# Mamba scan block: order of matmuls, vector work and activations within a tile, and where the scan's carry is kept

## The reference: what is computed

```
u  = silu(conv(in_proj_u(x)));  z = in_proj_z(x)
dt, B, C = split(x_proj(u));    dt = softplus(dt_proj(dt) + dt_b)
h[d,n] = exp(dt[d]*A[d,n]) * h[d,n] + dt[d]*u[d] * B[n]     # one step of time
y[d]   = sum_n h[d,n]*C[n] + u[d]*D[d]
out    = out_proj(y * silu(z))
```

## Time and profile before

| | |
|---|---|
| median of 3 runs | 1975.07 us (1973.82 to 1977.28) |
| profiled execution | 1973.6 us, of which the span from first to last instruction is 1971.8 us |
| busy in the span | PE 1445.4 us (73%), DVE 1359.6 (69%), POOL 1138.6 (58%), ACT 928.1 (47%) |
| granted TensorE clock, mean | 0.878 |
| Mamba block of layer 0, first to last scan | 56.5 to 588.6 us |
| Mamba block of layer 1, first to last scan | 1069.5 to 1602.2 us |

### The profile page before, as it was taken

The page is one execution under the profiler, slowest core; times in us unless marked ns, Lnnn a source line. Parts: engine busy times, 40 slices in busy tenths (PEclk is TensorE's granted clock), DMA queues, the critical chain, the costliest instruction groups (busy, mean ns, idle before and its releaser), DMA issues. The chain is left out here.

```text
span 1971.8 us, 28551 instructions
## 1 busy us (share of the span) xinstructions
PE 1445.4 (73%) x7776; PEld 980.9 (50%) x7777; DVE 1359.6 (69%) x1913; ACT 928.1 (47%) x1695; POOL 1138.6 (58%) x788
## 2 busy tenths in 40 slices
PE   6666766667656599999956766666667662799993
PEld 4333333333314499999834333333333222799992
DVE  2899999999995422222143999999999967444443
ACT  6666677667743011111136666677666731011111
POOL 0687788888880244444302888888878850355540
PEclk9889898998968699999968788998998866899996
DMA  3655566555638110111034565566555634111114
GB/s 110 147 135 121 129 144 146 125 126 134 145 79 354 54 41 32 38 37 36 26 126 98 129 138 121 129 143 139 134 121 135 148 136 188 38 48 48 47 41 152
DMA packets 75964, 217.61 MB, mean 110 GB/s; under 512 B 11856, under 2 KB 27408, under 8 KB 72592
## 3 DMA queue, kind: packets, MB, share of 16 engines
q1 hardware_dynamic: 67664, 194.53, 38.9%
q0 software_dynamic: 8256, 22.56, 3.5%
HBM read 178.34 MB, written 38.70 MB: 110 GB/s over the span
## 5 line engine op out<-in xcount | busy, mean ns | idle before, releaser
L669 POOL TENSOR_TENSOR L_hc<-L_h,L_cbq 128x1536 f32<-128x1536 f32 x192 | 660.1, 3438 | 210.6 <-DVE L_h L587 207.5
L492 ACT ACTIVATE ps<-L_dwq,L_negA 128x384 f32<-128x384 f32 x768 | 426.7, 574 | 227.4 <-DVE L_h L587 215.5
L364 PE MATMUL ps<-L_hc,same 128*32 128x384 f32 x1536 | 190.0, 571 | 238.9 <-POOL L_hc L669 238.9
L574 DVE TENSOR_TENSOR L_dbu<-L_dwq,ps 128x768 f32<-128x768 f32 x288 | 270.7, 941 | 29.4 <-DVE L_carry L649 13.1
L587 DVE TENSOR_TENSOR_SCAN L_h<-ps,L_h,L_dbu 128x384 f32<-128x384 f32 x288 | 275.0, 1002 | 12.9 <-ACT ps L492 12.8
L587 DVE TENSOR_TENSOR_SCAN L_h<-ps,L_carry,L_dbu 128x384 f32<-128x384 f32 x288 | 274.2, 1001 | 6.5 <-DVE L_dbu L574 4.7
L364 PEld LDWEIGHTS ps<-L_hc,same 128*32 128x32 f32 x1536 | 31.5, 113 | 358.2 <-POOL L_hc L669 324.3
L1151 DVE COPY Xn<-L_w 128x2048 f32 x86 | 107.6, 1253 | 117.1 <-PE ps L1101 108.3
L1134 ACT ACTIVATE L0e_hT<-ps 128x512 f32<-128x512 f32 x86 | 51.3, 597 | 267.2 <-PE ps L1101 267.2
L678 POOL TENSOR_TENSOR L_dbp<-L_dwq,L_cbq 128x768 f32<-128x768 f32 x96 | 175.1, 1824 | 0.0
L323 PE MATMUL ps<-Xn,L_fold 128*128 (+1 forms) x480 | 103.3, 368 | 89.2 <-DVE L_dw L595 89.2
(11 more groups left out here) (278 smaller groups left out, 2301.4 us busy)
## 6 DMA issues: line engine op xcount, KB each, us to landing
L_dwq<-dw_rows SPq DMA_DIRECT2D x192, 384.0 KB, 6.2
L_cbq<-cb_rows SPq DMA_DIRECT2D x192, 240.0 KB, 9.9
dw_rows<-L_dw SPq DMA_DIRECT2D x48, 384.0 KB, 2.3
L_w<-in_up SPq DMA_DIRECT2D x16, 1024.0 KB, 11.7
L_w<-in_down SPq DMA_DIRECT2D x8, 1024.0 KB, 26.6
tok_rows<-Xn SPq DMA_DIRECT2D x6, 768.0 KB, 13.1
L0s_got<-results SPq DMA_DIRECT2D x18, 256.0 KB, 2.9
L1s_got<-results SPq DMA_DIRECT2D x18, 256.0 KB, 3.5
```

The costliest lines, as they stand in the source:

```text
L364: mm = nc.tensor.matmul(y_ps[g * QW:(g + 1) * QW, :], same[:, 0:QW], hc[:, (k % 2) * Q + g, :], start=False, stop=(k == Q - 1))
L492: nc.scalar.activation(da(r, c), dwq[:, r, c % Q, 0, :], ACT.Exp, scale=negA[:, 0, c:c + 1]).then_inc(sem["da"], 1)
L574: nc.vector.tensor_tensor(dbu[:, at:at + 2, :], dwq[:, r, 2 * i:2 * i + 2, 1, :], spread(b_ps(r, k)), ALU.mult).then_inc(sem["dbu"], 1)
L669: nc.gpsimd.tensor_tensor(hc[:, at:at + Q, :], h[:, Q * k:Q * k + Q, :], cbq[:, r, k, :].unsqueeze(1).to_broadcast([P, Q, T]), ALU.mult).t ...
```

## The change

Four edits in the Mamba block.

1. PE: `spread_b(t, r, 2)` goes from behind `u_in` to the head of the tile; `u_in` is split in two (parts 0 and 1, then parts 2 to 4) around `sum_y(t-1, 3)`; `z_in` goes behind `u_in`; `project_dt` and `project_bc` go ahead of `sum_y(t, 0)` and `spread_b(t+1, 0)`. `add_relu` and `add_log` are written at the end of a tile for tile t+2 instead of at the head for tile t+1 (and once ahead of tile 0).
2. DVE: `times_u` goes from behind scan 3 to behind scan 0, `gate` from behind scan 5 to behind scan 3.
3. ACT: the block of two table loads, `silu_z` and `silu_u` goes from behind decay 7 to behind decay 6 (`SILU_AT`).
4. `h` gets one more column per state, which holds the state after the global token. Even tiles read their initial column from `h` too: column T-1, or column T where an image begins. The copy and DVE's wait for it are gone, and `carry` is only a step of the set-up.

```diff
@@ mamba, buffers
-        carry = sb("carry", [P, 2, N])
+        carry = sb("carry", [P, N])
...
-        h = sb("h", [P, N, T])
+        h = sb("h", [P, N, T + 1])
@@ tensor block
             spread_b(0, 0, 1)
+            add_relu(1)
+            add_log(1)
             pe.wait_ge(s_tok, 7)
 
             def tile(t, r, img1, img2, more):
 
                 first = isinstance(t, int) and t == 0
+                spread_b(t, r, 2)
+                if more == 2:
+                    u_in(t + 2, img2, (0, 1))
+                if not first:
+                    sum_y(t - 1, 1 - r, Q - 1)
+                if more == 2:
+                    u_in(t + 2, img2, (2, 3, 4))
                 if more:
-                    add_relu(t + 1)
-                    add_log(t + 1)
                     pe.wait_ge(sem["bc_out"], t + 2)
                     wait(pe, sem["res"], t - 1)
                     z_in(t + 1, img1)
-                if not first:
-                    sum_y(t - 1, 1 - r, Q - 1)
-                if more == 2:
-                    u_in(t + 2, img2, range(5))
-                spread_b(t, r, 2)
                 skip(t, r)
-                sum_y(t, r, 0)
-                if more:
-                    spread_b(t + 1, 1 - r, 0)
                 if more == 2:
                     project_dt(t + 2, r)
                     pe.wait_ge(sem["zs"], t + 2)
                     project_bc(t + 2, r)
+                sum_y(t, r, 0)
+                if more:
+                    spread_b(t + 1, 1 - r, 0)
                 sum_y(t, r, 1)
...
                 sum_y(t, r, 2)
+                if more == 2:
+                    add_relu(t + 2)
+                    add_log(t + 2)
@@ scalar block
-                    if c == 7 and more:
+                    if c == SILU_AT and more:
@@ vector block, scan
-                first = h[:, c, T - 1:T] if slot is None else carry[:, slot, c:c + 1] if isinstance(slot, int) \
-                    else carry[:, bass.ds(slot, 1), c:c + 1].rearrange("p a n -> p (a n)")
-                nc.vector.tensor_tensor_scan(h[:, c, :], da(t % 2 if isinstance(t, int) else int(slot is None), c),
+                first = h[:, c, T - 1:T] if slot is None else h[:, c, T - slot:T - slot + 1] if isinstance(slot, int) \
+                    else h[:, c, bass.ds(T - slot, 1)]
+                nc.vector.tensor_tensor_scan(h[:, c, 0:T], da(t % 2 if isinstance(t, int) else int(slot is None), c),
@@ vector block, tile
                     scan(t, 2 * j, slot)
+                    if j == 0 and not last:
+                        times_u(t + 1, 1 - r, [(s_dw_row[r], 16 * (p + 1))])
                     scan(t, 2 * j + 1, slot)
-                    if j == 1 and not last:
-                        times_u(t + 1, 1 - r, [(s_dw_row[r], 16 * (p + 1))])
                     if not (isinstance(t, int) and t == 0):
-                        if j == 2:
+                        if j == 1:
                             gate(t - 1, 1 - r)
@@ vector block, pair
-                if not last:
-                    dve.wait_ge(sem["scan"], (2 * p + 2) * N)
-                    nc.vector.tensor_copy(carry[:, 1, :], h[:, :, T - 1]).then_inc(sem["carry"], 1)
-                    dve.wait_ge(sem["carry"], p + 2)
@@ gpsimd block, times_c
-                nc.gpsimd.tensor_tensor(hc[:, at:at + Q, :], h[:, Q * k:Q * k + Q, :],
+                nc.gpsimd.tensor_tensor(hc[:, at:at + Q, :], h[:, Q * k:Q * k + Q, 0:T],
```

More of the change, by code:

```diff
@@ L36 @@
 DA_RING = 3
+SILU_AT = 6
 PAD = 2
@@ L614, in _ @@
             dve.wait_ge(s_tok, 6)
-            nc.vector.tensor_tensor(carry[:, 1, :].rearrange("p (k g) -> p k g", k=Q),
+            nc.vector.tensor_tensor(carry[:].rearrange("p (k g) -> p k g", k=Q),
                                     m["ones"][:, 0:N].rearrange("p (k g) -> p k g", k=Q),
@@ L618, in _ @@
             dve.wait_ge(sem["carry"], 1)
-            nc.vector.tensor_tensor(carry[:, 0, :].rearrange("p (k g) -> p k g", k=Q),
-                                    carry[:, 1, :].rearrange("p (k g) -> p k g", k=Q),
+            nc.vector.tensor_tensor(h[:, :, T].rearrange("p (k g) -> p k g", k=Q),
+                                    carry[:].rearrange("p (k g) -> p k g", k=Q),
                                     ps[:, 5, Q:2 * Q].unsqueeze(1).to_broadcast([P, Q, Q]), ALU.mult).then_inc(s_tok, 1)
```

## The result

The changed kernel takes 2000.79 us (median of 4 runs, 1997.96 to 2006.85) against 1976.14 us (4 runs): a ratio of 1.013, 95% interval 1.0103 to 1.0158. It is slower by some 25 us, where 2017 us was forecast. The profiled execution took 1998.67 us with a span of 1996.8.

The account below looks back on a forecast made before the run. VectorE was taken to bound the kernel, at some 21.1 us of work a tile. 44 tiles x (23.35 - 22.37) = 43 us on top of the profiled 1973.6 us gave 2017 us, range 1988 to 2046.

Parts of the forecast that it names:

- That dt comes no earlier, and VectorE waits for it in nearly every tile: Ahead of `times_u`: DVE idles 1 to 3 us in nearly every tile, some 60 to 90 us in all.
- 12.43 us from scan 7 to dt at full clock: Chain from the end of scan 7 through POOL, PE and `take_dt` to the next tile's dt: 12.43 us, no link shortened.
- the term "I take 0" for the pitch: POOL reading `h` at pitch 385 instead of 384: 0 to 0.2 us a pass, 0 to 18 us in all, taken as 0.
- the circle: Loop of scan 7, POOL, PE, `take_dt`, `times_u` and scan 7 again, in which the delay of dt goes round.
- 10.07 us from `times_u` to scan 7: DVE from the start of `times_u` to the end of scan 7: 6.44 + 2.76 + 0.87 = 10.07 us in the new order.
- The stall ahead of scan 7, 0.3 us: DVE waits 0.3 us ahead of scan 7 for the decay behind the activation block; before, it waited ahead of scan 8.
- Half of the clock's excess, 0.5 us a tile: PE's dt matmuls: low clock makes the mean tile's dt about 1.0 us later; half, 0.5, is taken.
- The rival of the clock "as before or worse": Low clock on dt matmuls: 23.85 us a tile, +65, 2039 us; always low 24.55, +96, 2070; chance 0.30.
- The circle at full clock, 22.85 us: Mamba tile: 12.43 + 0.05 + 10.07 + 0.3 = 22.85 us against 22.37 before, 0.48 more.
- The removed 28.6 us are swallowed by the wait: DVE: 18.3 us for the copy and its wait plus 10.3 for the spread, all lost to the wait for dt.
- Sum: Over the loops, 44 tiles x (23.35 - 22.37) = 43 us more, 2017 us; ends cancel.
- the prediction's own sum for full clock: Rival, dt always at full clock: 22.85 a tile, 1995 us; without stall 22.55, 1982; chance 0.52 together with the forecast.

Follow-up runs that it names:

- a scan: Changed kernel with `times_u` one scan later, behind scan 1: 1971.27 us, ratio 0.999 to the kernel before.
- `dbp`: Changed kernel with both parts of `dbp` behind the first `times_c` on GpSimd: 1977.25 us, ratio 1.0023 to the kernel before.
- two sums: Changed kernel with the first two of dt's three sums (relu and log) ahead of the third `sum_y` on PE: 1941.13 us, ratio 0.9833 to the kernel before.
- the run with PE kept busy: Changed kernel with the next tile's first spread done four times and the second three times: 1966.62 us, ratio 0.9965 to the kernel before.

## Why the prediction was right, point by point

- *That dt comes no earlier, and VectorE waits for it in nearly every tile*: right, 44 of 44 tiles, 69.3 us where 60 to 90 were forecast, though 26 of the waits were 0.55 to 1.44 us long, near the lower end of the 1 to 3 us named. The experiments that shortened one link each (a scan, `dbp`, the clock, two sums) all shortened the tile.
- *12.43 us from scan 7 to dt at full clock*: 11.80 measured. The step that was mis-sized is the term "I take 0" for the pitch, between bounds of 0 and +0.2 us a pass: it was -0.27, twice in the circle, 24 us over 44 tiles. The bound from below left out a gain, and nothing in the trace before could show it.
- *10.07 us from `times_u` to scan 7*: 10.11 measured, with the stall in it.
- *The stall ahead of scan 7, 0.3 us*: nearly absent, the two scans there take 1.98 instead of 1.92 us. From the end of `take_dt` to the end of scan 7 the mean of the 44 tiles is 10.23 us where 10.42 was forecast, 0.2 us too high, 8 us in all.
- *Half of the clock's excess, 0.5 us a tile*: too little. Fast dt takes 3.7 us from the third `times_c` and the mean was 4.50, so 0.8; dt ran slow in 18 of 44 tiles, against 25 before. The low clock did fall on the second `sum_y` more (19 tiles against 13), behind 3.04 to 3.15 us of idle, as argued, but in 16 tiles it ran fast behind as much. The rival of the clock "as before or worse" did not come: the mean granted clock is 0.880 against 0.878.
- *The circle at full clock, 22.85 us, already slower than the 22.37 before*: wrong, and the forecast of the sign leaned on it. In the run with PE kept busy, where dt is fast in all 44 tiles, the mean tile is 22.09 us and the kernel 0.35% faster than the one before. The gain on GpSimd and the missing stall make the circle that much shorter. So the change loses time only because the low clock on dt, which VectorE's slack hid before, now counts.
- *The removed 28.6 us are swallowed by the wait*: right as it ran, with the clock's share in the circle. The rows give a little less for the copy and its wait, 13.1 + 22 x 0.18 = 17.0 instead of 18.3 us, since the 0.65 us of one wait was taken for the mean. In the old order the same edit brings 18 us net of the pitch's cost.
- *Sum*: 23.35 us a tile forecast, 22.90 measured. The errors are -0.54 for GpSimd, -0.2 for the stall and +0.3 for the clock. That the last took back a part of the other two is luck.
- *The range*: its lower end of 1988 us is said to take in full clock, but the prediction's own sum for full clock is 1995, or 1982 without the stall, so that end comes from no term.
- Not seen in the prediction: that edits 1 and 2 hang together, so that the wait can't be undone by putting `times_u` back.

## What to carry to other kernels

Before an instruction is moved ahead, look up when its latest input lands and what has hidden that lateness; here ScalarE's mean wait of 2.2 us for dt, which cost nothing before, was the sign of it. If the chain behind that input starts in the same loop, the loss comes back in every turn, and the cure is to take links out of the chain: matmuls whose inputs are there early belong ahead of the one that waits for the chain. Where short matmuls stand behind idle stretches in such a chain, as here behind some 2 to 3 us, repeated matmuls in the gap can pay for themselves: they took 34 us off the changed kernel, and 21 off the version with dt's sums early. And an edit that makes another instruction faster or slower by the way, as the pitch did, wants a run of its own before a difference is put down to the edit that was meant.

## What the runs showed of the hardware

- GpSimd multiplied 1536 fp32 elements (four rows of 384, the other input broadcast over the rows) in 3.17 us with the rows 385 elements apart, and in 3.44 us at 384 and at 416, in all 192 instructions of each run. What in the pitch of 385 does it was not tried further.
- Making that instruction 8% faster and nothing else made the kernel 0.6% slower. The low clock fell on `u_in` in 22 of 44 tiles instead of 7, and VectorE waited for the spread behind it in just these; about half of the loss lies in the tiles of the loops, and the rest is open.
- TensorE's matmuls were at the low clock behind idle stretches of 2.27 us and 1.93 us, and at full clock behind the same 2.27 us in the next tile and behind 2.61: the length of the last idle stretch alone doesn't tell.
